# VectorE's order in an attention slot: the cosine's part of Q ahead of the inverses of the row sums

## The reference

```python
x = layernorm(x + attention(x))     # this change lies here
x = layernorm(x + wkv(w, u, x, ctx))
x = layernorm(x + ffn(x))           # dense layer + top-2 low-rank experts

# attention: 16 heads of 128 channels, 4 key/value heads, causal
q, k = rope(x @ Wq + bq), rope(x @ Wk + bk)
v = x @ Wv + bv
scores = einsum("bgjtd,bjsd->bgjts", q, k) / sqrt(16)
wei = softmax(where(causal, scores, -inf))      # row maximum, exp, row sum, divide
out = einsum("bgjts,bjsd->bgjtd", wei, v) ... @ Wo + bo
```

## Time and profile before

| | us |
|---|---|
| median of three runs | 1581.77 (1580.96 to 1586.83) |
| the profiled execution, its own time | 1579.19 |
| its span, from the first to the last instruction | 1577.4 |
| TensorE busy with matmuls | 1534.2 (97%) |
| VectorE busy | 1326.1 (84%) |
| ScalarE busy | 1117.8 (71%) |
| GpSimd busy | 1005.0 (64%) |

### The profile page before, as it was taken

The page is one execution under the profiler, slowest core; times in us unless marked ns, Lnnn a source line. Parts: engine busy times, 40 slices in busy tenths (PEclk is TensorE's granted clock), DMA queues, the critical chain, the costliest instruction groups (busy, mean ns, idle before and its releaser), DMA issues.

```text
span 1577.4 us, 32696 instructions
## 1 busy us (share of the span) xinstructions
PE 1534.2 (97%) x10492; PEld 1396.1 (89%) x10492; DVE 1326.1 (84%) x3435; ACT 1117.8 (71%) x2995; POOL 1005.0 (64%) x853
## 2 busy tenths in 40 slices
PE   8999999999999999999999999999999988989998
PEld 7899999999999999999999999999899977878786
DVE  6776688889889888898898989898989897877964
ACT  6877787877787878787878787878787865234333
POOL 2555586757676767676767667676767563644644
PEclk9999999999999999999999999999999998999999
DMA  7776444424441444244424441445144522112121
GB/s 245 243 256 209 156 144 141 129 67 152 148 144 50 154 153 141 62 154 154 141 61 149 142 159 48 125 151 180 48 128 154 167 65 97 58 68 94 60 89 54
DMA packets 81641, 202.62 MB, mean 128 GB/s; under 512 B 10432, under 2 KB 11072, under 8 KB 81472
## 3 DMA queue, kind: packets, MB, share of 16 engines
q1 hardware_dynamic: 81472, 200.53, 40.3%
HBM read 120.80 MB, written 37.75 MB: 101 GB/s over the span
## 4 chain that ended last, share of the span: by engine, by line
PE 81%; DVE 9%; issue 3%; POOL 2%; ACT 2%; DMA 1%; DVEq 1%; SPq 0%; POOLq 0%; ACTq 0%
PE bank L546 24%; PE bank L548 23%; PE bank L547 23%; PE bank L670 5%; PE bank L615 2%; DVE ED L1366 1%; PE bank L616 1%; PE bank L653 1%; PE bank L661 1%; DVE PS L1325 1%; DMA SW<-QB 1%; PE bank L685 1%; DVE OTl L1269 1%; ACT Xh L768 0%; DVE RO L1280 0%
## 5 line engine op out<-in xcount | busy, mean ns | idle before, releaser
L546 PE MATMUL bank<-Xh,W 128*128 128x256 f32 x1280 | 357.4, 279 | 3.6 <-DVE Vl L1242 1.5
L548 PE MATMUL bank<-Xh,W 128*128 128x256 f32 x1280 | 356.2, 278 | 0.0
L547 PE MATMUL bank<-Xl,W 128*128 128x256 f32 x1280 | 355.8, 278 | 0.0
L1050 POOL TENSOR_TENSOR Ql<-RC,Qh 128x512 fp32r<-128x512 f32 x127 | 168.8, 1329 | 191.9 <-ACT Qh L768 191.7
L783 ACT ACTIVATE S<-S,NM 128x128 f32<-128x128 f32 (+1 forms) x512 | 229.0, 450 | 68.7 <-DVE NM L1181 67.7
L1038 POOL TENSOR_TENSOR SW<-SW,tables 128x512 f32<-128x512 f32 x128 | 175.4, 1370 | 125.0 <-DMA SW<-QB 125.0
L546 PEld LDWEIGHTS bank<-Xh,W 128*128 128x128 f32 x1280 | 241.5, 189 | 5.5 <-issue 2.8
L548 PEld LDWEIGHTS bank<-Xh,W 128*128 128x128 f32 x1280 | 241.2, 188 | 0.0
L547 PEld LDWEIGHTS bank<-Xl,W 128*128 128x128 f32 x1280 | 241.0, 188 | 0.0
L768 ACT ACTIVATE PTh<-bank 128x384 fp32r<-128x384 f32 x256 | 125.1, 489 | 148.7 <-PE bank L670 147.6
L768 ACT ACTIVATE S<-S,RL 128x128 f32<-128x128 f32 (+1 forms) x512 | 204.4, 450 | 31.7 <-DVE RL L1188 31.3
(11 more groups left out here) (161 smaller groups left out, 4428.1 us busy)
## 6 DMA issues: line engine op xcount, KB each, us to landing
W<-kept SPq DMA_DIRECT2D x140, 512.0 KB, 4.5
SW<-QB SPq DMA_DIRECT2D x256, 128.0 KB, 2.3
kept<-W SPq DMA_DIRECT2D x40, 512.0 KB, 4.8
XR<-XR SPq DMA_DIRECT2D x64, 128.0 KB, 2.3
RO<-in_xn SPq DMA_DIRECT2D x16, 512.0 KB, 4.0
KVT<-in_ctxt SPq DMA_DIRECT2D x16, 512.0 KB, 4.8
mixed<-RO SPq DMA_DIRECT2D x16, 512.0 KB, 4.5
XR<-in_xt SPq DMA_DIRECT2D x15, 512.0 KB, 4.2
```

Of the source, the lines that this page charges most:

```text
L546: nc.tensor.matmul(dst, lhs[0], rhs[0], start=first, stop=False)
L547: nc.tensor.matmul(dst, lhs[0], rhs[1], start=False, stop=False)
L548: return nc.tensor.matmul(dst, lhs[1], rhs[0], start=False, stop=last)
L1050: gp.tensor_tensor(Q[1][:, :, :], RC[:, i % 2, :, :], Q[0][:, :, :], ALU.subtract).then_inc(q_lo, 1)
```

## The change

VectorE's slot takes the cosine's part of Q first and the inverses behind it. No instruction is added or removed, no wait is added or removed, and no other engine's queue changes.

```diff
             def slot(n):
                 first_sums(n, 0)
+                cosines(n)
                 inverses(n)
-                cosines(n)
                 first_sums(n, 1)
```

## The result

The kernel with the cosine first takes 1587.12 us (median of 19 runs, 1585.27 to 1588.94); the kernel before, on the same chip, 1581.6 us (19 runs, 1579.02 to 1586.83). The ratio is 1.0035, 95% interval 1.0028 to 1.0042 (by the medians 5.5 us). The bound that the prediction set for what can be told from no change, 0.5%, was wider than the measurement turned out to be; by it this is "no change", and by the runs it is a real loss. The median lies 0.1 us above the top of the stated range, 1587. One execution of a run further down, e6_short_before, took 3057 us in the slow state and is left out of its ratio.

A forecast was written before the change was run, and what follows sets the result against it. The prediction took TensorE to bound 100 to 1268 us and VectorE 1268 to 1310. To the profiled 1579.19 us it added -0.3 + 0 + 0 + 0.5, about 1579.4; the median, 2.6 us above, gave 1582.0, range 1579 to 1587.

The forecast's parts named there:

- the inverse doesn't overlap: Rival on VectorE: the inverse doesn't overlap the cosine, making VectorE later in every slot; 1587 us, chance 0.10.
- scores wait for Q: Rival: the late inverse delays ScalarE's Kh or Qh and GpSimd's Ql, so scores start late; 13 us, 1595, chance 0.05.
- the kept gain: Rival: TensorE's waits for the cosine shrink by 1.95 us and the end stretch gains 0.8; 1579.2 us, chance 0.07.
- The end: Term for the VectorE-bound stretch, 1268 to 1310 us: +0.5 us, between -0.8 and +2.1.
- The inverse behind a cosine that waits for QB: Term for VectorE's 60 slots waiting for QB: inverse loses idle-time cover, costed at 0; 6 us without other cover.
- The clock: Rival: the clock's fall near 1290 to 1294 us moves, 1.2 us either way, 1580.8 or 1583.2; inside the forecast.
- The inverse comes later: Term: in late slots VectorE's inverse is 0.38 us later, at most 0.65, hidden by slack; 0, bounds 0 and 3 us.
- So neither kind reaches TensorE: Claim that slack between Ql and the scores, or between inverse and normalisation, hides the late inverse from TensorE; taken as 0.
- seldom lives to the next slot: Claim that ScalarE's waits for the maxima and for TensorE absorb a lateness of 0.38 us.
- nothing but the number of TensorE's columns counts: Claim for 100 to 1268 us, three quarters of the run: TensorE, busy 1165.82 of 1168 us, alone sets the time.
- The cosine comes earlier: Term: the cosine gains 0.02 to 0.15 us in late slots, shrinking TensorE's 13 waits; -0.3 us, bounds -2.0 and 0.

The follow-up runs named there:

- e6_short_before: Kernel before, with GpSimd's low part of Q (Ql) cut to 4 of 256 columns: 1585.3 us, ratio 1.0027.
- e16_full_before: Kernel before, GpSimd's large operations cut to 4 columns, VectorE filled with added reciprocals of 60 columns and statistics over 512 columns: 1582.67 us, ratio 1.0008.
- e17_full_after: Changed kernel (cosine first), GpSimd's large operations cut to 4 columns, VectorE filled with added reciprocals and statistics: 1582.72 us, ratio 1.0006 to the kernel before.
- e10_free_before: Kernel before, GpSimd's large operations cut to 4 columns, reciprocals of 128x64 added on VectorE ahead of some scans and recurrence operations: 1570.16 us, ratio 0.9920.
- e8_not12: Changed kernel, but with the old order in the 16 slots 12 behind a start of a recurrence: 1586.01 us, ratio 1.0032 to the kernel before.
- e5_short_after: Changed kernel, with GpSimd's low part of Q cut to 4 of 256 columns: 1595.2 us, ratio 1.0094 to the kernel before.
- e4_before_qh: Kernel before, with ScalarE making Qh ahead of the normalisation in odd slots: 1590.43 us, ratio 1.0049.
- e13_qh13: Kernel before, with ScalarE making Qh ahead of the normalisation only in slots n % 16 == 13 (from 45 on): 1585.80 us, ratio 1.0021.

## Why the prediction was wrong

**Right.** The inverse is some 0.4 us later in late slots (0.38 predicted), and the cosine and the inverse overlap in the new order as in the old: 555.00, 555.30 and 555.38 are the starts of cosine, inverse and the operation behind. So the rival "the inverse doesn't overlap" is false, although its 1587 is the time that was measured: that is luck. The wait for the exponentials moved from the inverse to QB (35.5 to 74.1 us, 69 predicted). The scores and the transposes wait no more than before, so the rival "scores wait for Q" is false, too, as is "the kept gain". The end did not grow: from the scores of head 244 to the last instruction it takes 330.0 us before and 330.3 after, and from 1268 to 1310 VectorE's 39.39 us and TensorE's 35.53 lie beside 38.75 and 34.55 in the earlier trace rows, with the heads shifted by 6 us. The inverse behind a cosine that waits for QB, put at 0 with 6 us as its price without cover, cost nothing that e16_full_before and e17_full_after could show; that its price is near the loss is chance. The clock did not do it: it is 1.00 in the steady stretch in both, and the end's is 0.96 in both.

**The step that failed** is *The inverse comes later*, "I take 0; bounds 0 and 3 us". It measured about +5.8 us in the steady stretch. I followed the late inverse to ScalarE, to Ql and to the scores, found the slack there, and stopped, as if a Ql that is in time for its reader did nothing else. It does: while GpSimd works at it, VectorE's two-input operations stand still, VectorE comes late to its next results, and TensorE waits for the cosine or for the accumulators. "So neither kind reaches TensorE" was the sentence that failed. The rows needed were in the trace of before, which has the scan of line 1355 at 1.64 us in this slot and at 1676 ns in the mean, while 11 of the 55 scans of 128x514 take 1.22 us there (1.16 in the runs with GpSimd out of the way). The text never asked why one operation had several durations. The same step says that lateness "seldom lives to the next slot" on ScalarE: its wait for the inverse went from 24.3 to 69.5 us, +45, where I had 15, and from 39 times to 95. I had counted only the 39 slots that waited already; in the others the inverse had less slack than its lateness. Which of them stand behind a cosine that waits for QB isn't counted. ScalarE made up for most of the 45 in its other waits, for the maxima (61.7 to 32.9 us) and for the transposes (144.5 to 135.9), so the second of these, which was to give way, gave little.

**A second step failed ahead of it**: "nothing but the number of TensorE's columns counts" in the steady stretch. TensorE's 1165.82 busy us of 1168 are matmuls with modelled ends, and short stalls vanish in them. (Its busy time did not stay unchanged either: 1163.21 after.) Counting matmuls instead (8359 against 8411 in e10_free_before), the kernel before loses 7.2 us there already, and by the scores of heads 12 and 244 it loses 7.9. So TensorE stood at the edge of VectorE's pace in the crowded slots, and the 2.2 us that its matmuls wait in the earlier trace rows were the visible part of something over three times as large. *The cosine comes earlier*, -0.3 us, could not be kept either: in the slots that count the cosine came no sooner, and behind slot 109 it came 0.37 us later.

The chances follow from that: I had no rival in which a late Ql reaches TensorE over VectorE, and so gave a slower kernel too little.

**What stays open.** The stand-still is shown in single slots and, by e16 and e17 against the change, as the thing without which the order costs nothing. How the 5.8 us divide over the steps was tried for slots 14 and 30 (e8_not12): the first went, the second stayed, and where the lateness at 30 arises isn't known. Why a short Ql makes the order cost more (e5_short_after) is open. That the sooner Ql of e4_before_qh loses its 8.8 us by the same collisions is read from one slot of e13_qh13 and from slot 102; over half of the step at 27 goes another way, scores that wait for Ql, and the rest is argued.

## What to carry to other kernels

Before calling a delay harmless, ask not only who waits for the delayed result, but what its engine blocks while it works: where GpSimd and VectorE both work on SBUF, give each GpSimd operation a place in VectorE's order. One operation with several durations in the trace is the sign. And a TensorE that is 99.8% busy may still lose: count the matmuls in a stretch, or time from the same instruction of one head to that of a later one.

## What the runs showed of the hardware

A scan of 128x514 over two SBUF tiles took 1.16 us with GpSimd out of the way, and 1.64, 1.91, 2.03 and 2.12 us when a GpSimd operation was under way at its start, each time ending 1.09 us behind that operation's end, nearly its whole undisturbed time: it did next to nothing until then. In the kernel before, 44 of the 55 such scans from 100 to 1268 start under a GpSimd operation, and 42 of them end 1.08 or 1.09 us behind it. VectorE's products and sums of 128x512 over two tiles, 0.68 us alone, end 0.55 us behind in nearly every case. It isn't two tiles alone: the ED operation of line 1340, over one tile, takes 0.34 us alone and 1.12 in the mean under a GpSimd operation. The sum of line 1280, over a PSUM bank and one SBUF tile, takes 0.68 us with or without a GpSimd operation. The other way round, GpSimd gives way: its product SW of 128x512 took 1.30 us in one slot and 1.85 us in another, where its record starts together with that of VectorE's A2Z, which ran at its own pace there:

```profile
554.90 1.85 POOL L1038 TENSOR_TENSOR SW<-SW,tables 128x512 f32<-128x512 f32 x1 [1.24 <-DMA SW<-QB]
554.91 0.68 DVE L1362 TENSOR_TENSOR A2Z<-QS,ED 128x512 f32<-128x512 f32 x1
```

A2Z took 1.33 us where SW had come first (556.46 against 556.98). The Trainium skill, SBUF — State Buffer, section "SBUF: two separate sides", says that the pair of ports that the two engines share goes to whichever operation starts first, for the whole instruction, and that the other is blocked; it counts among these VectorE's operations with two SBUF inputs. The trace agrees where the starts lie apart; where they are 0.01 us apart in the record, it can't tell which came first. The prediction had drawn on the overlap of two VectorE instructions and not on this.

The runs also show how sensitive this tuned pipeline is to it: an inverse, and with it Ql, later by 0.4 us cost 5.5 us of 1582, a Qh moved ahead, which brings Ql 0.8 us sooner, 8.8 us, and a Ql cut short 4.4 us.
